# A post-LayerNorm transformer layer with banded attention: scores in runs of three, attention output turned to columns by DMA, FFN bias on ScalarE

## What is computed

```python
# x: (16, 512, 256) float32, 16 heads of 16, window W = 128
qkv = x @ Wqkv + bqkv
scores = q @ k_window.T / 16      # keys of the block before, the own and the next block
scores = where(|kpos - qpos| <= 128 and 0 <= kpos < 512, scores, -1e30)
a = softmax(scores) @ v_window
x = layernorm(x + a @ Wout + bout)
W1q, W2q = ternary(W1), ternary(W2)        # round(W / mean|W|), clipped to -1..1
h = relu(x @ W1q.T + b1)                   # 256 -> 1024
x = layernorm(x + h @ W2q.T + b2)
```

## Time and profile before

| | |
|---|---|
| median of three runs | 1186.8 us (1184.37 to 1189.89) |
| profiled execution | 1187.86 us, span 1186.1 us |
| TensorE busy | 1056.2 us, 89% (weight loads 65%) |
| VectorE busy | 859.3 us, 72% |
| ScalarE busy | 613.3 us, 52% |
| GpSimd busy | 518.8 us, 44% |
| mean granted TensorE clock | 0.924 |

### The profile page before, as it was taken

One profiled execution on the slowest core, in us unless ns is written; L12 is line 12 of the kernel. 1 busy time (PEld: TensorE's weight loads), 2 busy tenths in 40 slices (PEclk: granted clock), 3 DMA queues, 4 the chain that ended last, 5 costly groups with the idle time before them and its releaser, 6 DMA issues.

```text
span 1186.1 us, 23520 instructions
## 1 busy us (share of the span) xinstructions
PE 1056.2 (89%) x8132; PEld 771.9 (65%) x8132; DVE 859.3 (72%) x2934; ACT 613.3 (52%) x1258; POOL 518.8 (44%) x824
## 2 busy tenths in 40 slices
PE   4778899999989899998989999898989999897966
PEld 3444676766767576676767666676767667675755
DVE  3975777778787777778777777877777787777333
ACT  4154554655455564556455555545655554555421
POOL 2124353544535445463535445453535445344430
PEclk9677899998989999898999989898998989898889
DMA  5835255434354443444344534424554342442000
GB/s 169 108 54 92 28 82 82 68 70 73 58 75 68 83 73 76 61 80 65 56 82 73 88 61 78 75 37 82 82 82 68 69 74 57 57 69 56 1 19 18
DMA packets 56999, 81.49 MB, mean 69 GB/s; under 512 B 7729, under 2 KB 27697, under 8 KB 56882
## 3 DMA queue, kind: packets, MB, share of 16 engines
q1 hardware_dynamic: 56882, 80.00, 40.3%
HBM read 20.19 MB, written 8.39 MB: 24 GB/s over the span
## 4 chain that ended last, share of the span: by engine, by line
PE 77%; DVE 13%; issue 4%; POOL 2%; ACT 2%; DMA 1%; SPq 0%; POOLq 0%; DVEq 0%; ACTq 0%
PE shared L484 18%; PE st_a L459 13%; PE shared L503 12%; PE shared L595 11%; PE shared L582 10%; DVE mx L812 5%; PE st_b L459 5%; PE shared L578 3%; PE shared L564 3%; DVE oT_lo L859 2%; POOL ln_rstd L1007 1%; PE shared L543 1%; PE mx L475 1%; DVE qk_lo L839 1%; DVE rmax L812 1%
## 5 line engine op out<-in xcount | busy, mean ns | idle before, releaser
L812 DVE CUSTOM_DVE_ANT_0 mx<-mx,band 128x384 f32<-128x384 f32 (+1 forms) x1024 | 480.1, 514 | 187.0 <-PE mx L475 182.6
L670 ACT ACTIVATE probs<-st_a 128x384 f32<-128x384 f32 (+1 forms) x384 | 202.0, 526 | 371.3 <-PE st_a L459 367.7
L475 PE MATMUL mx<-k_stack,q_stack 48*128 48x384 f32 (+1 forms) x1024 | 273.0, 369 | 8.0 <-DMA k_stack<-qk_lo 3.9
L973 POOL TENSOR_SCALAR_AFFINE_SELECT probs<-probs 128x512 f32<-128x512 f32 (+1 forms) x256 | 128.8, 527 | 317.5 <-ACT probs L670 316.3
L670 ACT ACTIVATE probs<-st_b 128x384 f32<-128x384 f32 (+1 forms) x384 | 200.8, 523 | 0.0
L459 PE MATMUL st_a<-q_stack,k_stack 50*128 50x384 f32 (+1 forms) x512 | 186.9, 406 | 3.1 <-ACT probs L670 2.4
L475 PEld LDWEIGHTS mx<-k_stack,q_stack 48*128 48x128 f32 x1024 | 165.7, 201 | 13.2 <-DVE rmax L812 8.7
L503 PE MATMUL shared<-probs,v_aug 128*32 128x384 f32 (+1 forms) x2048 | 161.2, 445 | 0.7 <-DVE x L902 0.7
L459 PEld LDWEIGHTS st_a<-q_stack,k_stack 50*128 50x128 f32 x512 | 90.3, 197 | 104.2 <-issue 63.5
L812 DVE DVE_READ_ACCUMULATOR2_ANT rmax<- 128x1 f32 x1024 | 144.5, 141 | 0.0
L459 PE MATMUL st_b<-q_stack,k_stack 50*128 50x384 f32 (+1 forms) x512 | 143.2, 320 | 0.0
(11 more groups left out here) (107 smaller groups left out, 1965.3 us busy)
## 6 DMA issues: line engine op xcount, KB each, us to landing
q_stack<-qk_hi SPq DMA_DIRECT2D x128, 128.0 KB, 4.3
k_stack<-qk_hi SPq DMA_DIRECT2D x128, 128.0 KB, 5.2
x_raw<-in_xT SPq DMA_DIRECT2D x16, 512.0 KB, 5.7
q_stack<-qk_lo SPq DMA_DIRECT2D x64, 128.0 KB, 3.9
k_stack<-qk_lo SPq DMA_DIRECT2D x64, 128.0 KB, 5.5
y<-in_x SPq DMA_DIRECT2D x16, 512.0 KB, 6.1
out<-x SPq DMA_DIRECT2D x32, 256.0 KB, 2.1
probs<-in_w2T SPq DMA_DIRECT2D x1, 1024.0 KB, 10.6
```

Of the source, the lines that this page charges most:

```text
L475: mm = pe.matmul(PMX[i % N_MAX][:, col:col + n], SQ[rows, hd, W * m:W * m + W], SK[rows, hd, k0:k0 + n], start=True, stop=True)
L670: act.activation(PR[:, v % 2, g // 2, lo:lo + n], PST[i % 2][:, 0:n], ACT.Exp, scale=SCALE) \
L812: mx = dve.tensor_tensor_reduce(ps, ps, band, 1.0, -3e38, ALU.add, ALU.max, RMAX[:, g, m:m + 1])
L973: pool.affine_select(out=pr_before, in_=pr_before, compare_op=ALU.is_ge, fill=0.0, base=0, pattern=[[0, n], [1, W]], channel_multiplier=-1)
```

## The change

Scores get a third bank and the shared work loses one (3 + 3 + 2). Units come in runs of three. `nmt` writes to a bank of the maxima. `ut` and TensorE's part of `ot` are gone: v and the ones lie alternately in `VAUG`, so that u has o and its sums in alternate rows, and two transfers per quad (`columns`) take the even rows to `OC` and the odd ones (the sums, 16 times each) to `SC`, which is o transposed. The new step `od` takes the reciprocal of `SC` in place (128x512, twice per row) and multiplies, once on VectorE and once on GpSimd. ScalarE adds b1 in the relu (two activations into `H32`, then a copy to the high part), the remainder is made from `H32`, that of pair 1 on GpSimd. `x1` is wholly on ScalarE, LayerNorm 1's factors come in two halves, and several waits are split by half or by tile. `SIDE`, `LAG`, `RUNS_AT` are new, and SyncE follows a list, `TRANSFERS`.

```diff
 SIDE = [
-    [("qk", 0), "nmt", "pva", "pvb", ("vp", 0), "ut", ("vp", 1), ("ot", 0), ("ot", 1), ("qk", 1), ("op", 0),
-     ("op", 1)],
-    [("ln1", 0), ("ln1", 1), ("ln1", 2), ("qk", 2), "nmt", ("ln1", 3), "pva", "pvb", ("x1", 0), ("x1", 1),
-     ("x1", 2), ("x1", 3), "ut", ("x1t", 0), ("x1t", 1), ("qk", 3), ("f1", 0, 0)],
-    [("f1", 0, 1), ("xs", 0), "nmt", ("f1", 0, 2), ("xs", 1), ("f1", 0, 3), "pva", "pvb", ("f2", 0), "ut",
-     ("f1", 1, 0)],
-    [("f1", 1, 1), "nmt", "xr", ("ln2", 0), ("ln2", 1), ("f1", 1, 2), ("f1", 1, 3), "pva", "pvb",
-     ("f2", 1), "ut", ("ln2", 2), ("ln2", 3)],
+    ["nmt", "pva", "pvb", ("ot", 0), ("qk", 0), ("od", 1), ("qk", 1), ("ot", 1), ("vp", 0), ("vp", 1), ("op", 0),
+     ("ln1", 0), ("ln1", 1)],
+    [("op", 1), "nmt", ("x1", 0), ("ln1", 2), ("qk", 2), ("ln1", 3), ("x1", 1), ("qk", 3), ("x1", 2), ("x1", 3),
+     "pva", "pvb", ("x1t", 0), ("x1t", 1)],
+    ["nmt", ("f1", 0, 0), ("f1", 0, 1), ("f1", 0, 2), "pva", "pvb", ("f1", 0, 3), ("od", 0), ("f2", 0)],
+    [("f1", 1, 0), "nmt", "xr", ("f1", 1, 1), ("ln2", 0), ("ln2", 1), ("f1", 1, 2), "pva", "pvb", ("f1", 1, 3),
+     ("f2", 1), ("xs", 0), ("ln2", 2), ("ln2", 3), ("xs", 1)],
 ]
-N_MAX = 3
-RUN = 2
-RUNS_AT = (0.5, 0.92)
+BANKS = (3, 3)
+N_SCORE, N_MAX = BANKS
+REST_ON_POOL = (1,)
+X1_ON_DVE = ()
+RUN = 3
+RUNS_AT = (0.22, 0.89)
+
+TRANSFERS = (('columns', 0), ('stack', 3), ('maxima', 0), ('x', 0), ('maxima', 1), ('stack', 0), ('columns', 1), ('maxima', 2), ('stack', 1), ('columns', 2), ('residual', 0), ('columns', 3), ('maxima', 3), ('stack', 2), ('store', 0), ('store', 1))
...
+            def columns(r, vq):
...
+                i, q = vq // 2, 4 * r + vq
+                rows = slice(64 * (vq % 2), 64 * (vq % 2) + 64)
+                sp.wait_ge(s_u, q + 1)
...
+                sp.dma_start(OC[rows, i, :], U[0:P:2, :]).then_inc(s_uin, 16)
+                sp.dma_start(SC[rows, i, :], U[1:P:2, :]).then_inc(s_uin, 16)
...
                 if i == 0:
                     pe.wait_ge(s_stk[v], 96 * b + 96)
                     pe.wait_ge(s_nmin[v], 16 * b + 16)
...
+                    if v < 2 or stages(at)[2]:
+                        pe.wait_ge(s_stk[(v + 2) % 4], 96 * (b + v // 2) + 96)
...
-                    act.activation(HID[0][:, 2 * p:2 * p + 2, :].rearrange("p f t -> p (f t)"), G[:, :],
-                                   ACT.Relu).then_inc(s_hh, 1)
...
+                    for k, f in enumerate((2 * p, 2 * p + 1)):
+                        last = act.activation(H[:, 256 * k:256 * k + 256], G[:, 256 * k:256 * k + 256], ACT.Relu,
+                                              bias=B1C[:, f:f + 1])
+                    last.then_inc(s_hr, 1)
+                    act.wait_ge(s_hr, n + 1)
+                    act.activation(HID[0][:, 2 * p:2 * p + 2, :].rearrange("p f t -> p (f t)"), H[:, :],
+                                   ACT.Identity).then_inc(s_hh, 1)
...
+                elif name == "od":
+                    i = step[1]
+                    dve.wait_ge(s_uin, 128 * r + 64 * i + 64)
+                    dve.reciprocal(SC[:, i, :], SC[:, i, :]).then_inc(s_rc, 1)
+                    if i == 1:
+                        dve.wait_ge(s_rc, 2 * r + 2)
+                        dve.tensor_tensor(OC[:, i, :], OC[:, i, :], SC[:, i, :], ALU.mult).then_inc(s_od, 1)
...
+                elif step == ("od", 0):
+                    pool.wait_ge(s_rc, 2 * r + 1)
+                    pool.tensor_tensor(OC[:, 0, :], OC[:, 0, :], SC[:, 0, :], ALU.mult).then_inc(s_od, 1)
```

More of the change, by code:

```diff
@@ L122, with units_before @@
 WOVEN = weave()
+def units_before(v, step, kind):
+    return sum(k == kind for woven in WOVEN[v][:SIDE[v].index(step)] for _, k, _ in woven)
+NMT_AT = [units_before(v, "nmt", "max") for v in range(QUADS)]
+assert max(NMT_AT) < UNITS
 def stages(at):
@@ L179, in dve_order @@
                 due(maxima)
-        after = late[-1][0] + 1 if late and name_of(late[-1][1]) == name_of(step) in ("ln1", "ln2") else 0
+        after = late[-1][0] + 1 if late and name_of(late[-1][1]) == name_of(step) == "ln2" else 0
         late.append((max(maxima + LAG.get(name_of(step), 0), after), step))
@@ L412, in step @@
-                if post:
-                    store(b, 1)
+                for kind, v in TRANSFERS:
+                    if kind == "x" and nxt2:
+                        x_columns(b + 2)
+                        if at == -2:
+                            more_weights()
+                            sp.wait_ge(s_const, CONSTANTS)
+                    elif kind == "stack" and v == 3 and attn:
+                        stack(b, 3, at == 0)
+                    elif kind == "stack" and v < 3 and nxt:
+                        stack(b + 1, v, at == -1)
+                    elif kind == "store" and post:
+                        store(b, v)
+                    elif kind == "residual" and attn:
+                        residual(b)
+                    elif kind == "maxima" and row_of(v, "nmt", at) is not None:
+                        dr, vq = row_of(v, "nmt", at)
+                        maxima(b + dr, vq)
+                    elif kind == "columns" and row_of(v, "pvb", at) is not None:
+                        dr, vq = row_of(v, "pvb", at)
+                        columns(b + dr, vq)
@@ new lines, in x_columns, with residual, maxima @@
+            def x_columns(r):
+                if r > 0:
+                    sp.wait_ge(s_xl, r)
+                sp.dma_start(XRAW[:, :, :], xT[r:r + 1].rearrange("a (c p) t -> p (a c) t", p=P)).then_inc(s_x, 16)
+            def residual(r):
+                if r > 0:
+                    for t in range(TB):
+                        sp.wait_ge(*x1_done(r - 1, t))
+                sp.dma_start(Y[:, :, :], x[r:r + 1].rearrange("a (t p) d -> p (a t) d", p=P)).then_inc(s_xr, 16)
+            def maxima(r, vq):
+                q, c, ih = 4 * r + vq, vq // 2, vq % 2
+                sp.wait_ge(s_nmt, q + 1)
+                rows = SQ[64 * c + 48:64 * c + 50, 4 * ih:4 * ih + 4, :].bitcast(F32)
+                sp.dma_start(rows.rearrange("a g (n q) -> a (g n) q", n=NB), NMT[:, vq % 2].bitcast(F32)) \
+                    .then_inc(s_nmin[vq], 16)
@@ L471, in max_scores @@
                     pe.wait_ge(s_mxr, 12 * (4 * r + v) + i - N_MAX + 1)
+                if i == NMT_AT[(v + 2) % 4] and not (first and v == 0):
+                    pe.wait_ge(s_nmt, 4 * r + v)
                 for m in BLOCKS[u]:
@@ L751, in step @@
                             other_weights()
+                        row = row_of(v, step, at)
+                        before = name_of(step) in ("nmt", "ot", "pvb", "vp", "x1", "x1t", "xs")
+                        if row is not None and before:
+                            side_work(v, step, b, *row, at)
                         for _, kind, i in woven:
@@ L754, in step @@
                                 exp(b, v, i, at)
-                        row = row_of(v, step, at)
-                        if row is not None:
+                        if row is not None and not before:
                             side_work(v, step, b, *row, at)
@@ L871, in side_work @@
                         dve.wait_ge(s_mv2, 4 * r)
-                        dve.wait_ge(s_x1, 4 * r)
+                        for t in range(TB):
+                            dve.wait_ge(*x1_done(r - 1, t))
                     t = step[1]
@@ L890, in side_work @@
                         .then_inc(s_x1l, 1)
-                elif name == "f1":
+                elif name == "f1" and step[2] not in REST_ON_POOL:
                     hf, p = step[1], step[2]
```

280 lines of the change are left out of this document (127 added, 153 removed).

## The result

The changed kernel takes **1209.7 us** (median of four runs, 1207.9 to 1210.4), the kernel before, run beside it, 1186.0 us (1184.4 to 1189.9). The ratio is 1.019, with a 95% interval of 1.017 to 1.022: it is slower by 1.9%. 1095 us had been predicted. The profiled execution of after has a span of 1208.0 us.

The account below looks back on a forecast made before the run. TensorE was taken to bound the kernel, VectorE next. Per step, 53 us of work plus waits make 61.3, with 0.7 of clock 62.0 against 68.2; over 15 steps this gives 1095 us, range 1025 to 1195 (0.78).

Parts of the forecast that it names:

- first rival: VectorE's reciprocal of 128x512 is priced per element, 3.6 us instead of 0.68: step 67.8, 1182 us; chance 0.15.
- two dear rivals: VectorE's reciprocal at 3.6 us, 1182 us (0.15), or beyond 3.8 us each, making the kernel slower (0.16).
- each us counts twice: Both reciprocals delay VectorE where TensorE waits for maxima and qk1, so each us of length costs two a step.
- (a) to (c): TensorE work removed per step: FFN 1 bias matmuls 1.9 us, transposes of u 1.75, transposes of o 0.95.
- (d): Runs of three: 16 TensorE visits to the 64-row form for 24, saving 3.3 us a step (1.6 to 4.0).
- (1): SyncE's order: quad 2's stack transfer, behind columns and maxima, makes v0's first run wait 3.4 us a step (0 to 5).
- (2): xs moved from v2 to the end of v3: xT_lo's lateness hidden by the late stack, otherwise 3.2 us.
- (3): Column transfers of U, landing after 5.5 us (4 to 7): about 2 us of waiting in v0, 0.3 in v2.
- (4): Two shared banks for three, x1t followed at once by f1: 1.7 us at v2's start (0.8 to 3), 0.6 in v1.
- (5): Remainders and multiplication reading two SBUF tensors: 0.3 us a step (0 to 1).
- Hidden waits: Rival: stack lands in time, xs is served earlier, VectorE keeps up; step 57.5 us, 1027 us; chance 0.17.
- The change doesn't do what it says: Rival: 64-row visits stay dear or merge differently; step 63.7 us, 1120 us, inside the forecast's own range, no separate chance.

Follow-up runs that it names:

- experiment 11: Kernel with compact 32 x 128 reciprocals spread by four transfers: out projection moved to stage 1 and SyncE's list reordered; 1168.0 us, 0.985 of before.
- experiment 1: Changed kernel with each 128x512 reciprocal replaced by an ordinary VectorE pass (maximum of the sums with themselves); 1098.0 us, 0.924 of before.
- experiment 2: Changed kernel with each reciprocal over only 256 of the 512 columns; 1133.1 us, 0.954 of before.
- experiment 6: Kernel without reciprocals, stack and xs early (1072.7 us): runs of two pairs instead of three, VectorE's list no longer shifted by xs; 1141.1 us.
- experiment 3: Changed kernel with the stack transfer of quad 2 put ahead of the columns in SyncE's list; 1185.3 us, 0.999 of before.
- experiments 9 and 10: Changed kernel, stack and xs early, sums' reciprocals taken compactly and spread by transfers: 32 x 128 with four, 1167.8 us; 16 x 256 with two, 1183.6 us.

## Why the prediction was wrong

**The step that failed is the price of the reciprocal.** The text took 0.68 us, "since the row is no longer than its neighbour without division". A row of 16 elements could not tell. The three sizes measured, 3.348 us for 512 elements a partition, 1.747 for 256 and 0.931 for 128, lie on one line of 6.3 ns an element on some 0.13 us; by it 16 elements are 0.23 us, and the earlier trace rows has 0.249. The text's own reading in its first rival (0.141 off, the rest per element: 6.8 ns and 3.6 us) was right to 8%. The neighbour, a `TENSOR_SCALAR` with a mean of 0.326 us, misled: single ones take 0.25 us and up to 0.58 in before, the mean is 0.465 in after and 0.264 in experiment 11, so it is not the time of 16 elements of work. A row that allows both 0.7 and 3.6 us bears neither out, so the two dear rivals should have had more than 0.31.

**The second error is the rate, and in it the clock.** With 3.35 us the prediction's own rule gives 62.0 + 2 x 2.67 = 67.3 us a step, 1175 us, still faster than before; measured are 1209.7. So of the 115 us between forecast and result 80 are the price at the prediction's rate, 32 the rate, and 3 all the rest (experiment 1). For the waits alone the rate was rather too high: 25 us of idle time for each us of length (experiments 1, 2 and after) against 30. What the text left out of "each us counts twice" is the clock behind the waits: 44 us of busy time from experiment 1 to after, 8 in the first us and 36 in the rest. In the step shown the idle time grows by 3.8 us (69.93 - 60.58 against 63.10 - 57.57) and the busy time by 3.0, at a clock of 0.93 against 0.97. So its bound of 3.8 us, from which the kernel is slower, was too high: on the line between experiment 2 and after, 1186 us is reached near 2.9 us.

**The rest of the sum**, by experiment 1, where only this term is as it was forecast (step 62.0 forecast, 63.1 measured):

- *Removed work.* Busy time by granted clock is 63.44 x 0.95 = 60.3 us before and 57.57 x 0.97 = 55.8: 4.5 us gone, not 7.9 (over 500 to 920 us of both 3.7; over the whole executions, whose mean clocks are 0.924 and 0.927, TensorE is busy for 92.9 us less, 5.8 a row). A visit costs what was said: in experiment 1 a run of three takes 1.23 us, less 0.24 and 0.53 of slots, 0.46.

```profile
643.71 0.28 PE L626 MATMUL shared<-x1T_hi,w1q 128*128 128x256 f32 x1
...
644.72 0.39 PE L626 MATMUL shared<-x1T_lo,w1q 128*128 128x256 f32 x1
644.94 0.28 PE L626 MATMUL shared<-x1T_hi,w1q 128*128 128x256 f32 x1
```

  So (a) to (c) were put too high, or (d) gives less as work than in order of time (experiment 6 has 1.7 of 3.3); which, isn't settled. PV isn't it: its busy time rose from 161 to 178 us in all, but is 161.5 in experiment 3, so that was the clock behind the wait for the stack.
- *(1) The stack.* 2.85 us in the step of after, 47.9 in 16 in the sum; 3.4 was said. The walk through SyncE's list holds, and with it the place: last issue at 597.12, landing 5.4 us later.
- *(2) xs.* Hidden by (1), as said; with the stack in time, 44.3 us in 13 waits, 3.4 each (3.2 was said).
- *(3) The columns* land 2.8 us after their issue, not 5.5; the bound of 4 was too high as well. Two rows of the page, us to landing last:

```profile
k_stack<-qk_lo SPq DMA_DIRECT2D x64, 128.0 KB, 5.5
...
o_cols<-u SPq DMA_DIRECT2D x64, 128.0 KB, 2.8
```

  Both move 128 KB; one writes 16 partitions, the other 64, but the first is also the last of six issued in a row, so which of the two makes the difference isn't shown. With it the 2 us of (3) shrink: the reciprocal doesn't wait for its data (4.3 us in all), and in experiment 1 the waits for maxima are 11.9 us in the runs and 7.3 at `nmt`, 1.3 a step.
- *(4)* In experiment 1 TensorE idles 8.5 us in front of x1's transposes (L612) and 7.1 us behind them for x1T_hi, in 15 steps: 1.0 a step, where 1.7 was said (bounds 0.8 and 3).
- *(5) Operands in SBUF.* The remainder of the FFN takes 862 ns in the mean, where passes of its size take 0.69. The mean mixes two cases: in 300 us of after the median is 693 ns and the longest 1896. The long ones stand beside a GpSimd instruction that reads SBUF:

```profile
585.32 2.38 POOL L1049 TENSOR_TENSOR y<-y,bout_rep 128x1024 f32<-128x1024 f32 x1
587.07 1.18 DVE L944 TENSOR_TENSOR hid_lo<-hidden,hid_hi 128x512 fp32r<-128x512 f32 x1 [0.59 <-ACT hid_hi L795]
...
654.27 2.37 POOL L1049 TENSOR_TENSOR y<-y,bout_rep 128x1024 f32<-128x1024 f32 x1
655.29 1.90 DVE L944 TENSOR_TENSOR hid_lo<-hidden,hid_hi 128x512 fp32r<-128x512 f32 x1
```

  Both remainders end 0.55 us after the GpSimd instruction does (588.25 and 587.70, 657.19 and 656.64), whenever they began. The Trainium skill (SBUF — State Buffer, Who interferes with whom) says that a VectorE instruction with two inputs in SBUF and a GpSimd one that reads SBUF contend; these rows agree with it. On the path it is nearly nothing: in after TensorE waits for this remainder for 2.3 us in all, so the 0.3 us a step that was taken was enough. `neg_max` (465 ns for 326 in the earlier trace rows) and GpSimd's affine selects (725 and 660 ns) were longer too; what they stood beside wasn't looked at.
- *Clock.* 1.7 us a step in experiment 1 (57.57 x 0.03), not 0.7.

So the forecast's 62.0 is near 63.1 in part by chance: work 2.8 us too low, waits 2.8 too high (8.3 said, 5.5 idle), clock 1.0 too low. What was shown is that the change without its reciprocals would have gained 7.6%, that to put the stack first gives 24 us (experiment 3), and that the reciprocals took 112 us and with them the whole gain. *Hidden waits* was no case: (1) is there in every run that keeps its order. *The change doesn't do what it says* was none either: a step has 16 visits for 24, and runs of two are slower (experiment 6).

## What to carry to other kernels

An operation whose tile grows 32 times must be priced by its rate, not by its row at the small size; when the row allows 0.7 and 3.6 us, measure it alone first. A layout that repeats a number 16 times so that a later product is simple also repeats the division. On an engine that works in order, a long instruction costs twice over: by what stands behind it, and by the chain that goes through it; to cut it in parts helps only the first. And a wait has two prices, its length and the clock behind it: compare busy time for the same matmuls, beside idle time, before a difference is put down to waits.

## What was not expected of the hardware

- VectorE's `RECIPROCAL` is linear in the elements of a partition at 6.3 ns each on some 0.13 us (0.249, 0.931, 1.747, 3.348 us for 16, 128, 256, 512), and the number of partitions doesn't matter (32 x 128 takes 0.935 us, 16 x 256 1.735). An ordinary pass over 128x512 has 0.69. The Trainium skill (VectorE: DVE Perf Modes, First, the fixed hardware budget) gives a repeat count of 8; read as eight cycles an element it was an estimated 4.3 us in the prediction, and the measurement decides: 3.35.
- Transfers of 128 KB from SBUF to SBUF land after 2.8 us (the columns, into 64 partitions) and after 3.9 to 5.5 (the stacks, into 16, six in a row); the cause wasn't taken apart.
- Waits of TensorE of 2.85 and 2.99 us are followed by 3.3 and 3.8 us at 0.61 and 0.63 of the clock, which is 1.3 and 1.4 us more; one of 7.4 us by at least 4.1 us wholly at 1.2 GHz (0.50), 2.1 us more. In these two places the price of a wait of 3 us is about one and a half times its length. Over whole executions it isn't a constant: experiments 9 and 10 idle equally long, and TensorE's busy time differs by 22 us.
